# Weight means and the constant row from sums by VectorE, two buffers for turned units, last products by token halves, router sums by ScalarE

## The reference

```python
x = x + attention(layernorm(x), ctx, Wq, bq, Wk, bk, Wv, bv, Wo, bo)
h = layernorm(x)
scores = softmax(h @ G)                     # 8 experts
w = scores where among the top 2, else 0
gate, up = silu(h @ gate_w), h @ up_w       # 8 experts x 32 units
out = (gate * up * w) @ down_w + ((h @ lora_A) * w) @ lora_B
x = x + out
```

## Time and profile before

| | us |
|---|---|
| median of 3 runs | 117.26 (117.11 to 117.43) |
| the profiled execution, its own time | 117.28 |
| its span, first to last instruction | 115.5 |
| TensorE busy | 108.6 (94%) |
| VectorE busy | 91.4 (79%) |
| ScalarE busy | 70.2 (61%) |
| GpSimd busy | 49.4 (43%) |

### The profile page before, as it was taken

The page is one execution under the profiler, slowest core; times in us unless marked ns, Lnnn a source line. Parts: engine busy times, 40 slices in busy tenths (PEclk is TensorE's granted clock), DMA queues, the critical chain, the costliest instruction groups (busy, mean ns, idle before and its releaser), DMA issues.

```text
span 115.5 us, 2328 instructions
## 1 busy us (share of the span) xinstructions
PE 108.6 (94%) x892; PEld 82.3 (71%) x892; DVE 91.4 (79%) x192; ACT 70.2 (61%) x115; POOL 49.4 (43%) x79
## 2 busy tenths in 40 slices
PE   6999998999997999899999999999999999999780
PEld 6998677887885586586585766667778988586560
DVE  5436896999999997979999995899777998984410
ACT  0998528686878769895676796898427134313300
POOL 6929947499799920400052000222831674400000
PEclk9999999999999999999999999999999999999999
DMA  1999797474291002920000000000000000202022
GB/s 59 372 357 352 264 364 243 179 272 189 90 341 33 0 0 101 346 112 0 6 6 0 0 11 0 0 0 0 6 0 0 0 0 0 91 3 97 0 91 91
DMA packets 8453, 11.76 MB, mean 102 GB/s; under 512 B 697, under 2 KB 4986, under 8 KB 8442
## 3 DMA queue, kind: packets, MB, share of 16 engines
q1 hardware_dynamic: 7624, 10.83, 26.4%
q10 hardware_dynamic: 818, 0.79, 2.0%
HBM read 4.21 MB, written 1.05 MB: 46 GB/s over the span
## 4 chain that ended last, share of the span: by engine, by line
PE 61%; DVE 11%; ACT 7%; DMA 6%; SPq 5%; issue 4%; ACTq 2%; POOL 1%; POOLq 1%; DVEq 0%
PE unit L692 16%; PE unit L800 13%; PE unit L790 8%; PE unit L774 7%; DMA qstack<-q_lo 6%; PE unit L809 5%; PE unit L855 2%; PE unit L857 2%; PE unit L856 2%; DVE rowmax L616 2%; SPq L333 2%; ACT qstack L450 2%; PE unit L816 1%; ACT L450 1%; PE unit L842 1%
## 5 line engine op out<-in xcount | busy, mean ns | idle before, releaser
L616 DVE TENSOR_REDUCE rowmax<-unit 128x4 f32<-128x1024 f32 x32 | 37.6, 1221 | 3.5 <-PE unit L774 3.4
L502 ACT ACTIVATE probs<-unit 128x1024 f32<-128x1024 f32 x32 | 31.7, 1025 | 8.0 <-PE unit L790 7.3
L800 PE MATMUL unit<-probs,vaug 128*32 128x256 f32 x256 | 16.3, 384 | 0.0
L790 PE MATMUL unit<-qstack,kstack 64*128 64x256 f32 x128 | 13.1, 304 | 0.8 <-ACT probs L502 0.5
L774 PE MATMUL unit<-kstack,qstack 63*128 63x256 f32 x128 | 12.7, 302 | 0.8 <-DMA qstack<-q_lo 0.8
L790 PEld LDWEIGHTS unit<-qstack,kstack 64*128 64x128 f32 x128 | 9.2, 185 | 5.8 <-issue 2.9
L774 PEld LDWEIGHTS unit<-kstack,qstack 63*128 63x128 f32 x128 | 9.0, 185 | 4.2 <-issue 2.4
L435 POOL TENSOR_TENSOR x2T_lo<-x2T,x2T_hi 128x512 fp32r<-128x512 f32 x3 | 3.8, 1276 | 17.8 <-ACT x2T L517 17.8
L800 PEld LDWEIGHTS unit<-probs,vaug 128*32 128x32 f32 x256 | 7.1, 109 | 5.1 <-issue 0.2
L289 POOL TENSOR_TENSOR low<-low,weight_low 128x128 f32<-128x128 f32 x6 | 2.3, 402 | 14.5 <-DVE weight_hid L668 14.5
L692 PE MATMUL unit<-wf,x2T 128*128 128x136 f32 (+1 forms) x40 | 8.2, 344 | 0.0
(11 more groups left out here) (127 smaller groups left out, 222.6 us busy)
## 6 DMA issues: line engine op xcount, KB each, us to landing
kstack<-k_hi SPq DMA_DIRECT2D x8, 256.0 KB, 3.2
qstack<-q_hi SPq DMA_DIRECT2D x8, 256.0 KB, 3.0
xs<-x SPq DMA_DIRECT2D x4, 256.0 KB, 4.6
kstack<-k_lo SPq DMA_DIRECT2D x4, 256.0 KB, 2.4
qstack<-q_lo SPq DMA_DIRECT2D x4, 256.0 KB, 3.5
out<-xs SPq DMA_DIRECT2D x4, 256.0 KB, 2.1
wf<-wffn SPq DMA_DIRECT2D x1, 648.0 KB, 7.2
cT<-ctxT ACTq DMA_DIRECT2D x2, 256.0 KB, 4.9
```

Source lines behind the costliest of these rows:

```text
L502: act.activation(probs[:, n % NPAIR], unit[BANK["attn", b, i] // 2][:], ACT.Exp, scale=SCALE)\
L616: dve.tensor_reduce(rowmax[:, b % 2, :, :, i].rearrange("p t j -> p j t"), unit[BANK["max", b, i] // 2][:], AX.X, ALU.max).then_inc(done[" ...
L790: ins = pe.matmul(pair[:, j, t], kstack[b][rows, i, t * P:(t + 1) * P], qstack[b][rows, i], start=True, stop=True)
L800: ins = pe.matmul(dst[QUAD * j:QUAD * (j + 1), i % 2], vaug[:, b % NVALUE, t, 4 * i + j], probs[:, n % NPAIR, j % 2, t], start=(t == 0), s ...
```

## The change

1. **Weight means.** New stages on VectorE, `wsl` (136 columns) and `ws` (512 columns), add the two halves of the weights' rows; `mlow` and `mean` are then one product each. The sums lie in the buffers `low` and `hid`, which are not in use yet.
2. **Constant row.** New stage `bw` on VectorE, three instructions, makes the terms of Wo bv + bo; `bias` is then one product with a matrix of ones. The copy `bp` moves from VectorE to ScalarE.
3. **Router.** `r1` loses its last instruction (the factor 1/std goes into ScalarE's `ex` as its scale, one instruction per token half, which sum up the exponentials too), and `r3` loses its first.
4. **Two buffers** for the parts of turned x (x2T_hi, x2T_lo) and for the turned units (hidT, lT); the second ones lie in wk_hi, wk_lo, k_whole and q_whole, which are free by then. `x2hi`, `x2lo`, `hTE`, `lTE` wait for the element before the last and not for the last.
5. **Last element.** `glu:3.0` goes ahead of `down:1` and to bank 6; `down:3`, `res:3` and `out:3` are done by token halves (TILES), in two banks and two DMAs.
6. **Order of VectorE at the start:** `kfill:2`, a fill of 2048 columns, moves from ahead of `wlc` to behind `wfc`; `st1:3` moves behind it. At the end `res:1` moves behind `wh:3`. NWARM goes from 13 to 11.

```diff
-NWARM = 13
+NWARM = 11
+TILES = [[(0, 1)], [(0, 1)], [(0, 1)], [(0,), (1,)]]
 "tensor":
-        hT:1@1 lT:2@5 glu:3.1@2 hT:2@3 down:1@4 glu:3.0@2 lT:3@3 down:2@0 hT:3@1 down:3@0
+        hT:1@1 lT:2@5 glu:3.1@2 hT:2@3 glu:3.0@6 down:1@4 lT:3@3 down:2@0 hT:3@1
+        down:3.0@2 down:3.1@5
 "scalar":
-        ... qhi:0 xTE:1 n1:2 khi:1 ...
+        ... qhi:0 xTE:1 bp n1:2 khi:1 ...
 "vector":
-        ... klo:0 kfill:2 wlc qlo:0 st1:2 st1:3 bp wfc mx:0.0-2 ...
+        ... klo:0 wsl ws bw qlo:0 wlc st1:2 wfc kfill:2 st1:3 mx:0.0-2 ...
-        r3:2 h:2.1 res:0 h:2.0 r2:3 r1:3 h:3.1 r3:3 wl:3 res:1 h:3.0 wh:3 res:2 res:3
+        r3:2 h:2.1 res:0 h:2.0 r2:3 r1:3 h:3.1 r3:3 wl:3 h:3.0 wh:3 res:1 res:2 res:3.0-1
...
+        x2T_hi, x2T_lo = [sb("x2T_hi", [P, KT, S], F32R), wk_hi], [sb("x2T_lo", [P, KT, S], F32R), wk_lo]
+        hidT = [sb("hidT", [P, EF // P, S]), k_whole]
+        lT = [sb("lT", [P, S]), q_whole[:, 0]]
...
+                if name == "bw":
+                    dve.wait_ge(wo_in, 16)
+                    link(dve.tensor_scalar(bo_terms, wo[:, 0, 0:D], wo[:, 0, D:], None, ALU.mult))
+                    link(dve.scalar_tensor_tensor(out=bo_terms, in0=wo[:, 1, 0:D], scalar=wo[:, 1, D:], in1=bo_terms,
+                                                  op0=ALU.mult, op1=ALU.add))
+                    dve.wait_ge(bo_in, 16)
+                    dve.tensor_tensor(bo_terms[0:1], bo_terms[0:1], bo_row[:], ALU.add).then_inc(done["bw"], 1)
+                if name == "ws":
+                    wait_in(dve, wf_in)
+                    dve.tensor_tensor(wf_sum, wf[:, 0, 0:2 * EF], wf[:, 1, 0:2 * EF], ALU.add).then_inc(done["ws"], 1)
+                if name == "wsl":
+                    wait_in(dve, wf_in)
+                    dve.tensor_tensor(low_sum, wf[:, 0, 2 * EF:], wf[:, 1, 2 * EF:], ALU.add).then_inc(done["wsl"], 1)
...
-                    link(dve.tensor_tensor(below[:], logit, wide(top[:]), ALU.subtract))
-                    wait(dve, "rs2", b)
-                    dve.tensor_tensor(below[:], below[:], wide(rstd[:, 1, b]), ALU.mult).then_inc(done["r1"], 1)
+                    dve.tensor_tensor(below[:], logit, wide(top[:]), ALU.subtract).then_inc(done["r1"], 1)
...
+                    part = slice(TILES[b][i][0], TILES[b][i][-1] + 1)
+                    dve.tensor_tensor(xs[:, b, part], work[BANK["down", b, i]][:, part], xs[:, b, part], ALU.add)\
+                        .then_inc(done["res"], 1)
```

More of the change, by code:

```diff
@@ L68 @@
     "vector": """
-        warm edge kfill:0 st1:0 n1:0 st1:1 klo:0 kfill:2 wlc qlo:0 st1:2 st1:3 bp wfc mx:0.0-2 mx:0.4-5 mx:0.3
+        warm edge kfill:0 st1:0 n1:0 st1:1 klo:0 wsl ws bw qlo:0 wlc st1:2 wfc kfill:2 st1:3 mx:0.0-2 mx:0.4-5 mx:0.3
         mx:0.6-7 mx:1.0-6 mx:2.0 mx:1.7 mx:2.1 uT:0.0 mx:2.2 un:0.0 mx:2.3-5 uT:0.1 un:0.1 mx:2.6-7 x2:0 mx:3.0-1
@@ L431, in _ @@
                     wait(pool, "x2w", b)
[L432 to L435, removed]
+                    if b >= 2:
+                        wait(pool, "glu", b - 2, 0)
+                        wait(pool, "glu", b - 2, 1)
+                    if b % 2:
+                        for n in KV_PARTS:
+                            wait(pool, "k", n)
+                    pool.tensor_tensor(x2T_lo[b % 2][:], x2T[:, b % 2], x2T_hi[b % 2][:].bitcast(F32), ALU.subtract).then_inc(done["x2lo"], 1)
                 if name == "wl":
@@ L505, in _ @@
                     wait(act, "x2T", b)
[L506 to L510, removed]
+                    if b >= 2:
+                        wait(act, "glu", b - 2, 0)
+                        wait(act, "glu", b - 2, 1)
+                        wait(act, "x2lo", b - 2)
+                    if b % 2:
+                        wait(act, "wkl")
+                        for n in KV_PARTS:
+                            wait(act, "k", n)
+                    act.copy(x2T_hi[b % 2][:], work[BANK["x2T", b, 0]]).then_inc(done["x2hi"], 1)
                 if name == "x2w":
@@ L525, in _ @@
                     wait(act, "r1", b)
-                    act.activation(ex[:], below[:], ACT.Exp).then_inc(done["ex"], 1)
+                    wait(act, "rs2", b)
+                    for t in range(ST):
+                        ins = act.activation(ex[:, t], below[:, t], ACT.Exp, scale=rstd[:, 1, b, t:t + 1],
+                                             accum_out=esum[:, t:t + 1])
+                    ins.then_inc(done["ex"], 1)
                 if name == "th":
@@ L533, in _ @@
                         .then_inc(done["th"], 1)
+                if name == "bp":
+                    wait(act, "bias")
+                    act.copy(bo_sb[:], work[BANK["bias", 0, 0]][:, 0]).then_inc(done["bp"], 1)
                 if name in ("hTE", "lTE"):
                     wait(act, name[:2], b)
-                    if b:
-                        wait(act, "down", b - 1)
+                    if b >= 2:
+                        wait(act, "down", b - 2)
+                    if b % 2:
+                        for n in set(range(B)) - set(LOW_BY_VECTOR):
+                            wait(act, "klo", n)
+                            wait(act, "qlo", n)
                     if name == "hTE":
-                        act.copy(hidT[:], work[BANK["hT", b, 0]]).then_inc(done["hTE"], 1)
+                        act.copy(hidT[b % 2][:], work[BANK["hT", b, 0]]).then_inc(done["hTE"], 1)
                     else:
-                        act.copy(lT[:], work[BANK["lT", b, 0]][:, 0]).then_inc(done["lTE"], 1)
+                        act.copy(lT[b % 2][:], work[BANK["lT", b, 0]][:, 0]).then_inc(done["lTE"], 1)
         @block.vector
@@ L680, in _ @@
                 if name == "res":
[L681 to L682 removed]
+                    wait(dve, "down", b, i)
+                    part = slice(TILES[b][i][0], TILES[b][i][-1] + 1)
+                    dve.tensor_tensor(xs[:, b, part], work[BANK["down", b, i]][:, part], xs[:, b, part], ALU.add)\
+                        .then_inc(done["res"], 1)
         @block.tensor
```

53 lines of the change are left out of this document (19 added, 34 removed).

## The result

| | before | after |
|---|---|---|
| median, us | 117.26 (117.11 to 117.43) | 118.2 (118.02 to 119.59, 3 runs) |
| ratio to before | | 1.011, 95% interval 1.008 to 1.014 |
| the profiled execution, its own time | 117.28 | 118.20 |
| its span | 115.5 | 116.4 |

The change makes the kernel 0.9 us slower. The forecast of 117.4 is wrong, and 118.2 lies just outside the range; the time is that of the rival called late start, 118.05.

What follows compares the result with a forecast made beforehand. TensorE, full from about 30 us on, was taken as the bound, with gains only from stalls that go. 117.28 + 1.1 (start) - 0.94 (end) = 117.4 us; the range was 116.5 to 118.1.

Steps and rivals of the forecast that it cites:

- late start: Rival: VectorE starts the maxima at 21.5, each two-input instruction waiting out GpSimd; 118.05 us, chance 0.20.
- TensorE at the start: Ahead of max:0.0: fewer products and warming matmuls only make TensorE reach a DMA wait earlier; 0.
- VectorE at the start: VectorE's new order, with waits for GpSimd, starts mx:0.0 at 20.9 and not 18.92; a loss of 1.1 us.
- the upper bound: Latest forecast start of mx:0.0, 21.5, with GpSimd's L417 in the way too and waits of whole lengths; +1.7 us.
- From the first reduction to `mrow:0`: Eight reductions take 9.4 us, a late VectorE fills its waits, so mrow:0 comes at mx:0.0 + 9.4; +1.1 at 20.9.
- The middle: TensorE waits there for none of the two buffers, ex in two instructions or bp on ScalarE; 0.
- The end: Three gains behind the saturated stretch, from stalls, the last sum and the last store; -0.94 us, bounds -0.6 and -1.15.
- (a): TensorE's stalls at hT:1 and hT:2 shrink as VectorE comes earlier; -0.25 us, bounds 0 and -0.43.
- (b): Behind the last product only half of res:3 is left, about 0.41 instead of 0.69; -0.28 us.
- (c): The last store carries half the data; -0.41 us of the 2.1 to landing.
- the clock: Rival: TensorE's clock falls in the wider idle gap at the start, costing about 1 us; 118.4 us, chance 0.04.

Runs made afterwards that it cites:

- The probes: Separate kernels, no reference work: VectorE instructions of 256 columns, alone and beside GpSimd's; one input with a scalar per partition went from 348 to 1342 ns beside two-input ones.
- late fill alone: The kernel before with only kfill:2 moved, from ahead of wlc to just ahead of the first reduction: 118.27 us, ratio 1.0065.
- quiet GpSimd: The changed kernel with one wait more, GpSimd holding wv_lo back until VectorE's bw is done: 117.12 us, ratio 0.997 to the kernel before.
- without bw: The changed kernel with the constant row made by three products of TensorE, as before, instead of bw: 116.62 us, ratio 0.995 to the kernel before.
- v:1 moved: Kernel before plus the change's end, wsl, ws, bias behind xT:1, kfill:2 on ScalarE, st1:3 before wfc, q:1 before max:0.0, v:1 before max:0.2: 115.6 us.
- the end alone: The kernel before with the router's part, the two buffers and the order and halves of the last element: 116.03 us, ratio 0.987.

## Why the prediction was wrong

**TensorE at the start: right.** Its arrivals and the two warming matmuls cost nothing: `max:0.0` moved by 0.06, though q_lo's DMA was issued 1.36 later than before (15.96 against 14.60) and not 0.6. From its issue to `max:0.0` were 3.78 us before and 2.48 now. That reads as a queue ahead of it that had nearly run out: from 16 to 17 us the DMA engines were busy for 1.00 of the time before, and for 0.44 now.

**VectorE at the start: the term mis-sized, 21.4 and not 20.9.** The forecast let the first instruction of `bw` run at once, since it has one input in SBUF (0.41), and the waits of the other two end with wv_lo and cT_hi. In fact the first one waited, 0.96, which pushed the second past wv_lo into cT_hi and the third past that into cT_lo (1.36). The waits come one after another because each instruction of the chain of three finds the next of GpSimd's already running. L661's row had shown the wait only for two inputs; the step from "this row has two inputs" to "one input is free" had no row. The Trainium skill has the answer on the page cited (page "SBUF — State Buffer", section "Who interferes with whom"): a `tensor_scalar` or a copy can run in a mode that takes both of VectorE's ports, and then shuts GpSimd out or is shut out by it for the whole instruction. The probes agree: 0.35 to 1.34, and 0.66 beside fills, which don't slow two inputs. By that rule the first instruction of `bw` had to wait too, and the start lay near the upper bound. That bound, 21.5, had been built from another wait, for L417, and that one didn't come: `wsl`, with two inputs in SBUF, began at 10.67 beside it (L426 now, 10.28 to 11.00, two columns) and was over in 0.30. There the trace doesn't bear out a wait for the whole instruction, and the nearness of 21.5 to 21.40 is in part luck.

**From the first reduction to `mrow:0`: the step that failed.** The forecast read VectorE's three waits for TensorE, before, as room: 9.4 us of reductions in 10.3. Only two waits lay among the eight reductions, 0.24 and 0.18 us. The other 0.35 lay behind the last of them, 28.85 to 29.20, where TensorE still had `max:1.0` and `max:1.1` to do. After the change 0.40 and again 0.35 are left (26.39 + 4.82 = 31.21, `mrow:0` at 31.56). All of this is waiting for TensorE's own work. From `v:1` on (21.88 before) TensorE works without a stop to `mrow:0`: 7.32 us before, 7.35 after (24.21 to 31.56). `max:0.4`, ahead of it, needs the bank that `mx:0.1` has read. So a late `mx:0.0` moves the whole row. The rows of before that say so are the following, and they were to be seen in the timeline:

```profile
21.52 2.36 DVE L616 TENSOR_REDUCE rowmax<-unit 128x4 f32<-128x1024 f32 x2 [0.24 <-PE unit L774]
...
21.88 0.51 PE L692 MATMUL unit<-wv_hi,cT_hi 128*128 128x256 f32 x2
...
28.53 0.74 PE L774 MATMUL unit<-kstack,qstack 63*128 63x256 f32 x8
```

| kernel | first reduction | `mrow:0` | shift of each |
|---|---|---|---|
| before | 18.92 | 29.20 | |
| late fill alone | 20.00 | 30.08 | +1.08, +0.88 |
| quiet GpSimd | 19.83 | 29.96 | +0.91, +0.76 |
| without bw | 19.98 | 30.11 | +1.06, +0.91 |
| after | 21.40 | 31.56 | +2.48, +2.36 |
| v:1 moved | 19.09 | 28.67 | +0.17, -0.53 |

The shift passes nearly whole in four kernels, 0.12 to 0.2 of it lost. The last one shows the cause by taking it away: with `q:1` and `v:1` out of TensorE's row, `mrow:0` comes earlier than before though the first reduction is 0.17 later. With this step right and the start at 20.9 as forecast, the term is +1.8 (1.98 less 0.15) and the time 118.2, outside the range already; the start at 21.4 adds 0.5, and what the end gave beyond its term takes 0.45 off again. So the failed conversion is 0.7 of the error of the start term, the mis-sized start 0.5.

**The middle: right.** The shift at `hT:0` is 2.28 (86.40 against 84.12), within 0.1 of that at `mrow:0`; TensorE passed it on.

**The end: right in kind, 1.4 and not 0.94.** By the runs: the router's part 0.49 (117.41 to 116.92), the buffers and the order together 0.27 (to 116.65), of which the order nothing, the halves 0.62 (to 116.03). The kernel before had medians of 117.30 to 117.44 in these batches, so the split is good to about 0.15. In the profiled runs (a), the stalls, was under-sized. Taken from `hT:0` on (its weight load at 84.11 before, 84.23 in the end alone, 86.39 after the change) to the first product of `down:3` (109.28, 108.75, 110.91), the gain is 0.65 in both kernels, beyond the bound of 0.43. With the router's part alone it is 0.42 (84.34 and 109.09), about the whole of that bound, and the second buffers add 0.2. The stall ahead of `hT:1` is gone, that ahead of `hT:2` went from 0.93 to 0.35, and that ahead of `down:3` from 0.77 to 0.68. (b) is 0.27, as forecast. (c), the half store, is 0.4 (2.1 to 1.7 from issue to landing), as forecast. Together (b) and (c) are about 0.7 in the profiled runs, and the halves measured 0.62.

**The rivals.** The late start came, for the reason given there and one that wasn't. Its 118.05 took the start at 21.5 and the wrong conversion, and two errors cancelled: 0.7 too little at the start, 0.45 too little gain at the end. Its nearness to 118.2 is luck. The chance of 0.04 for the clock was low: one of the three runs after was at 119.59, with a mean clock of 0.986.

## What to carry to other kernels

Before a late engine is given credit for its waits, ask whom it waited for: if the other engine worked without a stop meanwhile, the wait was not room, and the delay passes nearly whole. Work moved to VectorE must be priced with what GpSimd does at that moment, and a chain of short dependent instructions is the worst case, as each can wait out one of GpSimd's; here 1.3 us became 3.1. And a fill that costs nothing in an idle stretch costs, behind the last input of the critical chain, whatever is longer than the wait that stood there; here 2.14 us met a wait of 0.94, and the first reduction came 1.08 later.
